# Adding the identity to the diagonal blocks of W1 and W2: accumulating DMAs in place of GpSimd tensor operations

## The chip, the core and the metric

The kernel runs on one core of one Trainium2 chip. The metric is the device time in microseconds (us) of one execution. Three executions of the kernel before took 483.61, 483.93 and 484.32 us, a median of 483.93 us. All views below are of one profiled execution of it.

## What is computed

Four residual layers follow each other on `x` of 8 batches by 256 rows by 1024 columns, in float32:

```
x = x + quantise(x)                       # L0: 8 groups of thresholds, deltas, zero points
x = x + einsum('bsi,boi->bso', x, W1[ids_a[b]])   # L1: one of 8 matrices 1024x1024, by batch
x = x + einsum('bsi,oi->bso', x, W2) + 0.5 * (x @ lora_A[ids_b[b]]) @ lora_B.T      # L2
x = x + (x @ B[ids_a[b]].T) @ A[ids_a[b]].T       # L3, rank 16
```

`x + x W` is computed as `x (W + I)`: each layer's residual is folded into its matrix by adding 1 to the diagonal. That addition is what the change touches.

## The kernel before

The rows of a batch are two halves of 128 (`t` = 0 and 1); a half is a "unit", of which there are 16. The five engines run programs of their own, written out by hand, which wait for one another on semaphores.

**ScalarE and VectorE (ACT, DVE)** walk through steps `n`, eight to a unit, one for each quantisation group. In a step ACT scales and rounds (`multiple`, L329, into the ring `tq` of 4) and makes a mask (`exceeds`, L344), and DVE takes the magic number off (`value`, L439), clamps (`clamp`, L448) and selects into `y` (`select`, L460). After a unit's last step `close_unit` (L468, L475) writes `x1`, the input of layer 1. Other work is put between the steps by tables of step numbers. Those that matter here are `ACT_W2` = steps 9 to 16, at which ACT rounds a slice `k` of W2 to `w2h` (L400), `DVE_W2` = steps 10 to 13 and 18 to 21, at which DVE takes the rest `w2l` (L513), and `ACT_X2`/`DVE_X2`, at which the result of layer 1 is split into `x2h` (L353) and `x2l` (L481).

**TensorE (PE)** first prepares the small adapter tables, then goes through the batches (`batch`). For each half it multiplies `x1` by `w1b` (`w1_x1`, L603, eight output tiles `o`, two to a pair `j`) and then `x2` by W2 (`product`, L628, in three terms: `w2h` by `x2h`, `w2h` by `x2l`, `w2l` by `x2h`). Before it uses pair `j` of W1 for the first half it waits for `w1_ready`. The first batch is written out, batches 1 to 6 are a loop (`pe.Fori`), the last is written out again. In each trace a float32 matmul of L603 leaves two records.

**SyncE (SP)** issues all loads and stores. W1 of a batch comes in four pairs of 1 MB into `w1b`, each as soon as PE has finished with the pair of the batch before (`w1_used`). W2 comes once, in eight slices of 512 KB, into a ring `stage` of `ST` = 4 buffers (`ua` and three of `ring`). Slice `k` + 4 can be loaded only when DVE has made `w2l` of slice `k` (`load_w2`, L211).

**GpSimd (POOL)** has one job after its two memsets: it adds `eye` (the identity, 128x128) to the diagonal blocks. `w2_diagonal(k)` (L290) waits for the load of slice `k`, and adds to one block of 128x128. `w1_diagonal(b, j)` (L295) waits for the load of pair `j` of batch `b`, and adds to two such blocks. For batch 0 the two kinds alternate; for batches 1 to 7 a loop does the four pairs. ACT waits for `w2_diag` before `w2h` of slice `k`. In a fragment:

```
if n in ACT_W2:
    k = ACT_W2.index(n)
    act.wait_ge(w2_diag, k + 1)
    nc.scalar.activation(w2h[:, k, :], stage[k % ST], ACT.Copy).then_inc(w2h_ready, 1)
```

Of the kernel before, what the change touches and what calls it, by code (L numbers as in the profile page):

```python
# [5 lines left out]
def quantised_residual_adapter_stack(nc, x, params, w1, w2t, w2n, b3t, b2n, b2r, a3, la, ids_b, ids_a,  # L6
# [9 lines left out]
    ALU = mybir.AluOpType  # L16
    ACT = mybir.ActivationFunctionType

    P = 128
    B, _, UN, KT, _ = x.shape  # L20
    T = UN * P
    OT = KT
# [11 lines left out]
    PAIRS = OT // 2  # L34
# [8 lines left out]
    TQ, MK, ST = 4, 2, 4  # L43

    ctx = ExitStack()
    with ctx:
        def sb(name, shape, dt=f32):
            return ctx.enter_context(nc.sbuf_tensor(name, shape, dt))
# [4 lines left out]
        def sem(name):  # L53
            return ctx.enter_context(nc.semaphore(name))
# [34 lines left out]
        eye = sb("eye", [P, P])  # L89
# [41 lines left out]
        y_ready = sem("y_ready")  # L131
        y_cut = sem("y_cut")
        x1_ready = sem("x1_ready")
        w1_ready = sem("w1_ready")
        w1_used = sem("w1_used")
        bank0_done = sem("bank0_done")
        acc_done = sem("acc_done")
        out_ready = sem("out_ready")
        w2_diag = sem("w2_diag")
        x2h_ready = sem("x2h_ready")  # L140
        x2l_ready = sem("x2l_ready")
        vh_ready = sem("vh_ready")
# [24 lines left out]
        def e_place(e):  # L167
            h, half = divmod(e, 2)
            return outb[:, h, half * DH:(half + 1) * DH]
# [111 lines left out]
        @block.gpsimd  # L281
        def _(pool):
            nc.gpsimd.memset(v_hl[:, :, :].bitcast(f32), 0.0).then_inc(pads, 1)
            nc.gpsimd.memset(u_hl[:, :].bitcast(f32), 0.0).then_inc(pads, 1)
            pool.wait_ge(b_in, 64)

            def w2_diagonal(k):
                pool.wait_ge(stage_in[k % ST], 16 * (k // ST + 1))
                diag = stage[k % ST][:, k * P:(k + 1) * P]
                nc.gpsimd.tensor_tensor(diag, diag, eye[:, :], ALU.add).then_inc(w2_diag, 1)  # L290

            def w1_diagonal(b, j):
                pool.wait_ge(w1_in[j], 16 * (b + 1))
                diag = w1b[:, 2 * j:2 * j + 2, 0:P]
                nc.gpsimd.tensor_tensor(diag, diag, eye[:, :].unsqueeze(1).to_broadcast([P, 2, P]), ALU.add) \  # L295
                    .then_inc(w1_ready, 1)

            for j in range(PAIRS):
                w1_diagonal(0, j)
                w2_diagonal(j)  # L300
            for k in range(PAIRS, KT):
                w2_diagonal(k)
            with pool.Fori(1, B) as b:
                for j in range(PAIRS):
                    w1_diagonal(b, j)

# [15 lines left out]
        def _(act):  # L322
# [67 lines left out]
            def tables(n):  # L390
                if n == ACT_G:
                    act.wait_ge(g_tiles, KT)
                    for i in range(2):
                        nc.scalar.activation(gsb[:, :, i * HALF:(i + 1) * HALF, :],
                                             g_bank[i][:, :].rearrange("p (i a r) -> p a i r", i=HALF, a=NA),
                                             ACT.Copy).then_inc(g_ready, 1)
                if n in ACT_W2:
                    k = ACT_W2.index(n)
                    act.wait_ge(w2_diag, k + 1)
                    nc.scalar.activation(w2h[:, k, :], stage[k % ST], ACT.Copy).then_inc(w2h_ready, 1)  # L400
                for e in range(2 * EH):
                    if n == ACT_E[e]:
                        act.wait_ge(e_done, 2 * EH)
                        nc.scalar.activation(e_place(e), e_bank[e][:, :], ACT.Copy).then_inc(e_ready, 1)  # L404
# [4 lines left out]
            for n in range(END):  # L409
                if n < STEPS:  # L410
                    multiple(n)
                if 2 <= n < STEPS + 2:
                    exceeds(n - 2)
                for i in range(2):
                    c, off = divmod(n - ACT_X2[i], G)
                    if off == 0 and 0 <= c < UN * B:
                        round_x2(c, i)
                for b in range(B):
                    s = n - PER * b
                    if s == ACT_V:  # L420
                        round_v(b)
                    if s in (ACT_U, ACT_U + 1):
                        round_u(b, s - ACT_U)
                    if s == ACT_LOW:
                        round_low(b)
                    for q in range(ACCS):
                        if s == ACT_OUT[q] and b < LAST:
                            finish_out(b, q)
                tables(n)
# [132 lines left out]
        def _(pe):  # L562
# [32 lines left out]
            def w1_x1(b, t, tiles):  # L595

                for o in tiles:
                    if t == 0 and o % 2 == 0:
                        pe.wait_ge(w1_ready, PAIRS * b + o // 2 + 1)
                    i = o // HALF  # L600
                    for k in range(KT):
                        at = (k - o) % KT * P
                        last = nc.tensor.matmul(x2_bank[2 * t + i][:, o % HALF * P:(o % HALF + 1) * P],  # L603
                                                w1b[:, o, at:at + P], x1[:, t, k, :],
                                                start=(o % HALF == 0 and k == 0), stop=(k == KT - 1),
                                                skip_group_check=True)
                    if t == 0 and o % HALF == HALF - 1:
                        last.then_inc(bank0_done, 1)
                    if t == 1 and o % 2 == 1:
                        last.then_inc(w1_used, 1)  # L610
# [34 lines left out]
            def batch(b, first=False, last=False):  # L645
                pe.wait_ge(x1_ready, UN * b + 1)
                if first:
                    w1_x1(b, 0, range(OT))
                else:
                    w1_x1(b, 0, range(U_AT))  # L650
                    for q in range(ACCS):
                        u_low(b - 1, q)
                    w1_x1(b, 0, range(U_AT, OT))
# [100 lines left out]
```

## Time and profile before

| | |
|---|---|
| median of 3 runs | 483.93 us (483.61 to 484.32) |
| profiled execution, first to last instruction (span) | 481.9 us |
| what the median has beyond that span | 2.0 us |
| PE / DVE / ACT / POOL busy | 464.9 / 419.4 / 358.6 / 45.5 us |
| POOL: 32 additions for W1, 8 for W2 | 36.5 us and 7.0 us of the 45.5 |
| mean DMA rate | 139 GB/s |

The profile gives no total time of its own for the profiled execution beside its span, so the 2.0 us is the difference to the median of other runs. "Busy" is time in which an instruction of the engine was being executed. A row of a timeline reads: start in us from the start of the span, duration in us, engine, line, operation, what it writes and reads, sizes and count, and in brackets how long the engine stood idle before and what released it.

### The profile page before, as it was taken

How to read it: one execution, taken by the hardware profiler on the slowest of the kernel's cores; microseconds unless marked ns; L12 is line 12 of the kernel's file. 1: busy time of each engine (PE TensorE's matmuls, PEld its weight loads, DVE VectorE, ACT ScalarE, POOL GpSimd, SP SyncE). 2: the span in 40 equal slices, each digit the busy share in tenths (PEclk: the TensorE clock that was granted, in tenths of full speed). 3: DMA queues.
4: the chain of work that ended last, by engine and by line, in shares of the span. 5: the costliest groups of instructions: out<-in, count | busy, mean ns of one | idle time of the engine just before them, and what ended most of it. 6: DMA issues, size and time to landing. Idle time of an engine off the chain costs nothing.

```text
span 481.9 us, 8215 instructions
## 1 busy us (share of the span) xinstructions
PE 464.9 (96%) x3184; PEld 424.7 (88%) x3184; DVE 419.4 (87%) x481; ACT 358.6 (74%) x383; POOL 45.5 (9%) x46
## 2 busy tenths in 40 slices
PE   3999869999999999999999999999999999999997
PEld 3969669898999989898999989898999989898995
DVE  5999999999999899989999899989999899989120
ACT  6979958678877879678877879678887879675011
POOL 1064000200002000200002000210003000100000
PEclk9999989999999999999999999999999999999999
DMA  7997214712335122712335122712335122702002
GB/s 282 407 415 258 113 34 149 294 54 97 131 127 212 44 95 97 294 44 103 131 120 218 44 89 101 294 44 103 131 101 237 44 86 104 294 2 88 1 1 87
DMA packets 17830, 67.07 MB, mean 139 GB/s; under 512 B 2576, under 2 KB 5904, under 8 KB 13712
## 3 DMA queue, kind: packets, MB, share of 16 engines
q1 hardware_dynamic: 17808, 66.81, 37.9%
q8 instruction: 10, 0.16, 0.2%
q14 instruction: 12, 0.10, 0.1%
HBM read 56.84 MB, written 9.96 MB: 139 GB/s over the span
## 4 chain that ended last, share of the span: by engine, by line
PE 90%; ACT 3%; DMA 3%; DVE 2%; issue 1%; POOL 1%; SPq 0%; DVEq 0%
PE x_bank L603 45%; PE acc L628 34%; PE acc L579 3%; PE x_bank L616 3%; PE acc L640 2%; PE acc L638 2%; DMA w1b<-w 2%; DMA rows<-own_rows 1%; ACT mask L344 1%; ACT w2h L400 1%; DVE y L460 1%; PE acc L567 1%; ACT tq L329 1%; PE acc L577 0%; ACT outb L404 0%
## 5 line engine op out<-in xcount | busy, mean ns | idle before, releaser
L603 PEld LDWEIGHTS x_bank<-x,w1b 128*128 128x128 f32 x2048 | 233.2, 193 | 8.2 <-issue 4.9
L603 PE MATMUL x_bank<-x,w1b 128*128 128x128 f32 x2048 | 234.8, 276 | 3.7 <-DVE x L475 3.7
L344 ACT ACTIVATE mask<-absx,negtop 128x1024 bf16<-128x1024 f32 x112 | 128.4, 1146 | 40.3 <-DVE y L460 39.5
L329 ACT ACTIVATE tq<-xin,magic,rdelta 128x1024 f32<-128x1024 f32 x128 | 157.0, 1234 | 0.6 <-DVE yhigh L526 0.3
L460 DVE COPY_PREDICATED y<-mask,uq 128x1024 f32<-128x1024 int16 x112 | 151.1, 1349 | 0.1
L439 DVE TENSOR_SCALAR tq<-tq,par 128x1024 f32<-128x1024 f32 x128 | 99.2, 775 | 3.7 <-DVE y L460 3.1
L448 DVE TENSOR_SCALAR uq<-tq,ylow,yhigh 128x1024 f32<-128x1024 f32 x112 | 92.3, 824 | 0.2 <-DVE y L460 0.2
L628 PE MATMUL acc<-w2h,x2h 128*128 128x512 f32 x256 | 80.9, 393 | 2.0 <-DVE x2l L481 2.0
L628 PE MATMUL acc<-w2h,x2l 128*128 128x512 f32 x256 | 79.9, 390 | 0.0
L628 PE MATMUL acc<-w2l,x2h 128*128 128x512 f32 x256 | 79.2, 390 | 0.0
L295 POOL TENSOR_TENSOR w1b<-w1b,eye 128x256 f32<-128x256 f32 x32 | 36.5, 1140 | 368.9 <-DMA w1b<-w 368.9
L628 PEld LDWEIGHTS acc<-w2h,x2l 128*128 128x128 f32 x256 | 48.1, 188 | 10.3
L628 PEld LDWEIGHTS acc<-w2l,x2h 128*128 128x128 f32 x256 | 48.0, 188 | 10.2
L628 PEld LDWEIGHTS acc<-w2h,x2h 128*128 128x128 f32 x256 | 46.3, 188 | 10.6 <-DVE x2l L481 2.4
L481 DVE TENSOR_TENSOR x2l<-x_bank,x2h 128x512 fp32r<-128x512 f32 x32 | 22.1, 690 | 35.5 <-ACT x2h L353 35.5
L353 ACT ACTIVATE x2h<-x_bank 128x512 fp32r<-128x512 f32 x32 | 18.9, 592 | 28.1 <-PE x_bank L603 27.8
L337 ACT ACTIVATE absx<-xin 128x1024 f32<-128x1024 f32 x15 | 15.9, 1063 | 21.9 <-DVE uq L468 21.9
L388 ACT ACTIVATE outb<-acc 128x512 f32<-128x512 f32 x32 | 18.1, 598 | 7.5 <-PE acc L640 7.5
L468 DVE SCALAR_TENSOR_TENSOR uq<-absx,top,y 128x1024 f32<-128x1024 f32 x16 | 23.2, 1448 | 0.6
L475 DVE TENSOR_TENSOR x<-xin,uq 128x1024 f32<-128x1024 f32 x16 | 19.4, 1215 | 0.0
L579 PE MATMUL acc<-x,w1b 128*128 128x128 f32 x128 | 16.8, 288 | 0.0
L616 PE MATMUL x_bank<-x2h,v_hl 128*128 128x256 f32 x64 | 16.3, 289 | 0.0
(57 smaller groups left out, 218.9 us busy)
## 6 DMA issues: line engine op xcount, KB each, us to landing
w1b<-w SPq DMA_DIRECT2D x32, 1024.0 KB, 6.7
xin<-x SPq DMA_DIRECT2D x16, 512.0 KB, 3.7
out<-outb SPq DMA_DIRECT2D x14, 512.0 KB, 2.8
w1b<-w2n SPq DMA_DIRECT2D x4, 1024.0 KB, 10.6
ring<-w2t SPq DMA_DIRECT2D x6, 512.0 KB, 6.7
ua<-e_dram SPq DMA_DIRECT2D x16, 128.0 KB, 2.5
ua<-w2t SPq DMA_DIRECT2D x2, 512.0 KB, 7.8
va<-la SPq DMA_DIRECT2D x8, 128.0 KB, 2.7
```

Of the source, the lines that this page charges most:

```text
L295: nc.gpsimd.tensor_tensor(diag, diag, eye[:, :].unsqueeze(1).to_broadcast([P, 2, P]), ALU.add) \
L329: nc.scalar.activation(tq[:, n % TQ, :], flat(xin, c % UN), ACT.Identity, bias=magic[:, 0:1], scale=rdelta[:, g:g + 1]).then_inc(t_ready, 1)
L344: nc.scalar.activation(mask[:, n % MK, :], absx[:, :], ACT.Relu, bias=negtop[:, g:g + 1], scale=1.0).then_inc(mask_ready, 1)
L439: nc.vector.tensor_scalar(tq[:, n % TQ, :], tq[:, n % TQ, :], -MAGIC, par[:, 1, g:g + 1], ALU.add, ALU.mult).then_inc(u_ready, 1)
L448: nc.vector.tensor_scalar(clamped_y, tq[:, n % TQ, :], ylow[:, g:g + 1], yhigh[:, g:g + 1], ALU.max, ALU.min).then_inc(clamped, 1)
L460: nc.vector.copy_predicated(y[:, :], mask[:, n % MK, :].bitcast(i16), uq[:, n % 2, :]) \
L468: nc.vector.scalar_tensor_tensor(ycut, absx[:, :], top[:, G - 1:G], y[:, :], ALU.is_gt, ALU.mult).then_inc(y_cut, 1)
L481: nc.vector.tensor_tensor(x2l[:, t, tiles, :].rearrange("p k t -> p (k t)"), x2_bank[2 * t + i][:, :], x2h[:, t, tiles, :].rearrange("p k ...
L579: last = nc.tensor.matmul(into, w2g[:, i, o * P:(o + 1) * P], b3s[:, o, :], start=False, stop=(o == OT - 1))
L603: last = nc.tensor.matmul(x2_bank[2 * t + i][:, o % HALF * P:(o % HALF + 1) * P], w1b[:, o, at:at + P], x1[:, t, k, :], start=(o % HALF == ...
L616: last = nc.tensor.matmul(low_bank[:, 0:T], v_hl[:, k, :], xs[:, :, k, :], start=(k == 0 and xs is x2h), stop=(k == KT - 1 and xs is x2l), ...
L628: nc.tensor.matmul(acc[2 * t + h][:, :], xs[:, t, k, :], w[:, k, h * DH:(h + 1) * DH], start=(k == 0 and xs is x2h and w is w2h), stop=Fal ...
```

## The change

The tensor operations of `w2_diagonal` and `w1_diagonal` become DMAs, issued by GpSimd, that read `eye` from the core's memory and add it to the block in place (`accum_op=ALU.add`). Since a DMA raises its semaphore by 16 in pieces, each W1 pair and each stage buffer gets a semaphore of its own. The waits of ACT and PE are rewritten to match, and GpSimd's loop over the batches is written out.

```
-        w1_ready = sem("w1_ready")
+        w1_ready = [sem(f"w1_ready{j}") for j in range(PAIRS)]
-        w2_diag = sem("w2_diag")
+        w2_diag = [sem(f"w2_diag{c}") for c in range(ST)]
...
             def w2_diagonal(k):
                 pool.wait_ge(stage_in[k % ST], 16 * (k // ST + 1))
                 diag = stage[k % ST][:, k * P:(k + 1) * P]
-                nc.gpsimd.tensor_tensor(diag, diag, eye[:, :], ALU.add).then_inc(w2_diag, 1)
+                pool.dma_start(diag, eye[:, :], accum_op=ALU.add).then_inc(w2_diag[k % ST], 16)
...
                 diag = w1b[:, 2 * j:2 * j + 2, 0:P]
-                nc.gpsimd.tensor_tensor(diag, diag, eye[:, :].unsqueeze(1).to_broadcast([P, 2, P]), ALU.add) \
-                    .then_inc(w1_ready, 1)
+                pool.dma_start(diag, eye[:, :].unsqueeze(1).to_broadcast([P, 2, P]), accum_op=ALU.add) \
+                    .then_inc(w1_ready[j], 16)
...
-            with pool.Fori(1, B) as b:
+            for b in range(1, B):
                 for j in range(PAIRS):
                     w1_diagonal(b, j)
...
-                    act.wait_ge(w2_diag, k + 1)
+                    act.wait_ge(w2_diag[k % ST], 16 * (k // ST + 1))
...
-                        pe.wait_ge(w1_ready, PAIRS * b + o // 2 + 1)
+                        pe.wait_ge(w1_ready[o // 2], 16 * (b + 1))
```

GpSimd's program from the end of its memsets on, before (a `w1b` row is a pair of W1, a `ua` or `ring` row a slice of W2):

```order
L284 MEMSET u_hl 128x1024
L295 ISA
L295 TENSOR_TENSOR w1b<-w1b,eye 128x2x128
L290 TENSOR_TENSOR ua<-ua,eye 128x128
L295 TENSOR_TENSOR w1b<-w1b,eye 128x2x128
L290 TENSOR_TENSOR ring<-ring,eye 128x128
L295 TENSOR_TENSOR w1b<-w1b,eye 128x2x128
L290 TENSOR_TENSOR ring<-ring,eye 128x128
L295 TENSOR_TENSOR w1b<-w1b,eye 128x2x128
L290 TENSOR_TENSOR ring<-ring,eye 128x128
L290 TENSOR_TENSOR ua<-ua,eye 128x128
L290 TENSOR_TENSOR ring<-ring,eye 128x128 x3
```

The same stretch now:

```order
L284 MEMSET u_hl 128x1024
L295 DMA w1b<-eye 128x2x128
L290 DMA ua<-eye 128x128
L295 DMA w1b<-eye 128x2x128
L290 DMA ring<-eye 128x128
L295 DMA w1b<-eye 128x2x128
L290 DMA ring<-eye 128x128
L295 DMA w1b<-eye 128x2x128
L290 DMA ring<-eye 128x128
L290 DMA ua<-eye 128x128
L290 DMA ring<-eye 128x128 x3
L295 DMA w1b<-eye 128x2x128 x28
```

The places and their order are the same; each addition has become a DMA, and the 28 of batches 1 to 7 follow without a loop.

TensorE's program at the head of the loop over batches 1 to 6, where it begins on a new W1, before:

```order
L599 ISA
L603 MATMUL x_bank<-x,w1b 128x128 x16
L599 REGISTER_ALU
L603 MATMUL x_bank<-x,w1b 128x128 x8
L638 MATMUL acc<-u_hh,low_hc 128x512
L640 MATMUL acc<-u_hl,low_lh 128x512
```

and now:

```order
L599 ISA
L603 MATMUL x_bank<-x,w1b 128x128 x24
L638 MATMUL acc<-u_hh,low_hc 128x512
L640 MATMUL acc<-u_hl,low_lh 128x512
```

No matmul has moved. The register additions that made each wait's number are gone from between them, since all four pairs now wait for the same number.

## Rows read from the trace of the kernel before

**Rows 1.** Page, chain that ended last: share of the span by engine.

```profile
PE 90%; ACT 3%; DMA 3%; DVE 2%; issue 1%; POOL 1%; SPq 0%; DVEq 0%
```

**Rows 2.** Waits, whole span: total us, times, longest us.

```profile
PE x_bank L603 <- DVE x L475: 3.7, 1, 3.7
...
ACT w2h L400 <- POOL ua L290: 2.8, 1, 2.8
...
PEld x_bank L603 <- DVE x L475: 2.2, 6, 0.4
```

**Rows 3.** Chain in order of time, stretch 25 to 66 us: start, us, what.

```profile
38.44 0.87 POOL ring L290
39.34 1.06 ACT w2h L400
...
54.84 0.49 ACT x2h L353
55.35 0.69 DVE x2l L481
...
64.28 1.15 DVE x L475
```

**Rows 4.** Timeline of ACT, the slices k = 0 and k = 4 of W2.

```profile
28.65 1.06 ACT L400 ACTIVATE w2h<-ua 128x1024 fp32r<-128x1024 f32 x1 [2.83 <-POOL ua L290]
...
42.95 1.04 ACT L400 ACTIVATE w2h<-ua 128x1024 fp32r<-128x1024 f32 x1
```

**Rows 5.** Timeline of POOL, the slices k = 0 and k = 4.

```profile
27.71 0.90 POOL L290 TENSOR_TENSOR ua<-ua,eye 128x128 f32<-128x128 f32 x1
...
42.00 0.52 POOL L290 TENSOR_TENSOR ua<-ua,eye 128x128 f32<-128x128 f32 x1 [2.69 <-DMA ua<-w2t]
```

**Rows 6.** Timeline of SP's DMA issues: slices k = 0, 3 and 4.

```profile
17.82 0.43 SPq L211 DMA_DIRECT2D ua<-w2t  x1
...
29.86 0.43 SPq L211 DMA_DIRECT2D ring<-w2t  x1
...
35.16 0.33 SPq L211 DMA_DIRECT2D ua<-w2t  x1
```

**Rows 7.** DMA issues from 17 to 30 us: count, KB each, median us to landing.

```profile
ring<-w2t SPq DMA_DIRECT2D x3, 512.0 KB, 8.4
ua<-w2t SPq DMA_DIRECT2D x1, 512.0 KB, 8.9
```

**Rows 8.** DMA issues from 35 to 46 us.

```profile
ua<-w2t SPq DMA_DIRECT2D x1, 512.0 KB, 6.8
...
vg<-g_dram SPq DMA_DIRECT2D x1, 64.0 KB, 3.7
```

**Rows 9.** All 8 loads of tile vg (64 KB each).

```profile
DMA to landing us min/median/max: 1.9/2.4/3.7
```

**Rows 10.** Timeline, DVE: first w2l, and L468 with POOL idle and busy.

```profile
33.38 1.75 DVE L513 TENSOR_TENSOR w2l<-ua,w2h 128x1024 fp32r<-128x1024 f32 x1
...
120.20 1.29 DVE L468 SCALAR_TENSOR_TENSOR uq<-absx,top,y 128x1024 f32<-128x1024 f32 x1
...
146.38 1.61 DVE L468 SCALAR_TENSOR_TENSOR uq<-absx,top,y 128x1024 f32<-128x1024 f32 x1
```

**Rows 11.** Timeline, POOL and PE: pair 1 of batch 1, and its use.

```profile
90.93 1.83 POOL L295 TENSOR_TENSOR w1b<-w1b,eye 128x256 f32<-128x256 f32 x1 [8.01 <-DMA w1b<-w]
...
96.27 5.62 PE L603 MATMUL x_bank<-x,w1b 128*128 128x128 f32 x48
```

**Rows 12.** POOL's additions for W1, all 32: min/median/max ns.

```profile
L295 POOL TENSOR_TENSOR w1b<-w1b,eye x32: 730/1001/2153, 25.6 to 422.1; 128x256 f32<-128x256 f32 x32
```

**Rows 13.** Stretches: length, busy PE, PEld, DVE, ACT, POOL; granted clock, DMA share, GB/s.

```profile
62.00:65.50 3.50, 0.00 (x0) 0.00 (x0) 3.43 (x5) 2.00 (x2) 0.00 (x0) 1.00 0.00 0
...
67.00:69.00 2.00, 2.00 (x12) 2.00 (x11) 2.00 (x4) 1.91 (x2) 0.00 (x0) 0.50 0.33 98
```

**Rows 14.** Chain in order of time: second half of batch 0 and of batch 1.

```profile
65.56 16.16 PE x_bank L603 x128
...
123.57 14.51 PE x_bank L603 x128
```

## The prediction

> **What bounds the kernel now.** I read the chain that ended last first, then the waits, then the timelines of the head. The chain lies on PE for 90% of the span [rows 1]. PE's waits show where it isn't PE: it stands still once for 3.7 us, for `x1` of the second unit, and its weight loads wait 2.2 us in all, six times, for the same line later on [rows 2]. GpSimd appears among the long waits once: ACT stood 2.8 us for the first slice of W2 [rows 2]. So two stretches are to be looked at. The head, up to PE's start on the second half at 65.56 us [rows 14], is where W2 is prepared and ACT and DVE set the pace. The batches after it, where PE does, are where only W1's additions take place.
>
> **The head, followed back.** The chain there goes from POOL's addition to slice k = 3, which ends at 39.31 us, to ACT's `w2h` at 39.34, then along ACT to `x2h` at 54.84, to DVE's `x2l` at 55.35, and along DVE to `x1` at 64.28 plus 1.15, for which PE has been waiting [rows 3]. A reader should see two things. ACT takes `w2h` of k = 3 0.03 us after POOL is done, so there is no reserve at that slice. And nothing on the chain between 39.34 and 65.43 is a transfer or a free engine: what ACT loses at a slice of W2 arrives at PE in full.
>
> **What the change does to the head.** Call A the time from the landing of a slice to the moment ACT sees its diagonal done. Now that is one POOL operation: 0.90 us at k = 0, 0.52 us at k = 4 [rows 5]. After the change it is the issue by GpSimd, the transfer of 64 KB within the core's memory, its addition, and the semaphore.
> - k = 0: issued by SP at 17.82, landed 8.9 us later, so at 26.7 [rows 6, 7]. ACT began at 28.65, having waited [rows 4]. ACT is delayed by 26.7 + A - 28.65, that is A - 1.9.
> - k = 3: issued at 29.86 [rows 6], landing by the median of its kind, 8.4 us [rows 7], at 38.3. ACT began at 39.34 [rows 3]. Delay A - 1.1.
> - k = 4: issued at 35.16 [rows 6], landed 6.8 us later [rows 8], at 42.0, where POOL took it up [rows 5]. ACT began at 42.95 [rows 4]. Delay A - 0.95.
>
> These are delays of one chain, so the largest counts, not their sum: D = A - 1.0. The later slices have several us between their addition and ACT's use and don't bind. This holds while the stage ring isn't held up in turn. Slice 4 can be loaded only after DVE's `w2l` of slice 0, which began at 33.38 [rows 10] where `w2h` of slice 0 was done at 28.65 + 1.06 = 29.7 [rows 4]: 3.7 us of reserve. With A - 1.9 above 3.7, so A above 5.6, each further microsecond counts about twice, once for slice 0 and again for slice 4.
>
> **The size of A.** The trace has no DMA of GpSimd and no accumulating one. The nearest rows are SP's loads of 64 KB: 1.9 us at the least, 2.4 at the median and 3.7 us in this very stretch, with other loads in flight [rows 8, 9]. From below A is 1.9 us; nothing lets a transfer that must first read both operands be quicker than the quickest plain one of its size. From above it is 8.9 us, what a load takes when it queues behind a full megabyte [rows 7]; the additions have a queue of their own. I take 3.7 us, the row nearest in size and stretch, and 0.7 us for a slower issue and the second operand. That 0.7 is my choice; half of it to three times it would do as well. A = 4.4 and D = 3.4 us.
>
> The Trainium skill ("DMA: Bandwidth & Descriptors", "Where the ~2 µs actually goes" and "Latency and other measured facts") gives about 2.0 us of fixed cost for a DMA issued by GpSimd and about 1 us to its first byte. By that, as an estimate from the page, A would be some 3.2 us and D 2.2; no run here shows a GpSimd DMA yet.
>
> **What the change does to the batches.** Each of the 28 additions becomes a DMA of 128 KB. The tightest is pair 1. It has landed by 90.93, when POOL takes it up, and PE needs it after two of three output tiles of the stretch that starts at 96.27 and lasts 5.62, so at 100.0 [rows 11]: 9.1 us for A. With A = 4.4 nothing waits. POOL's queue holds nothing else, so no one stands behind a slow issue except the next pair, which is needed later still. In batch 0 the pairs have about as much. Cost zero, covered by PE's work on the tiles before; the cover ends at A = 9.1.
>
> **What else is removed or added.** POOL's 36.5 us for W1 and 7.0 us for W2 of work go; nobody but ACT at k = 0 waited for them [rows 2]. They do slow DVE: L468 takes 1.29 us with POOL idle and 1.61 beside an addition, the first `w2l` 1.75 us [rows 10]. In the head that gives DVE back about 1 us, but ACT is what the chain runs on, so the gain is zero. In the batches DVE's gain is lost in its own wait for the next `x2h`. The register additions on PE lay between queued matmuls; zero. The traffic added is 6 percent of a megabyte load per slice and 13 per pair; zero.
>
> **Sum.** The span goes from 481.9 to 485.3 us. With the 2.0 us that the median of the runs lies above the span, 487.3 us, or 3.4 over the median of 483.93. A difference of 0.2% (about 0.97 us) is what a measurement of this kernel can tell from none.
>
> **Rivals.**
> 1. *DVE is freed and PE gets its x1 sooner* (faster). PE's weight loads wait for L475 six times, 2.2 us in all [rows 2], and additions of POOL stretch the DVE operations that lead to such an `x1`, as at 146.38 [rows 10]. If those waits are DVE's fault and the additions are what makes DVE late, up to 2.2 us go: 481.7 us. Against it: the waited-for `x1` is that of the second half, before which POOL is idle, and the head would have to cost nothing, so A would have to be 1.0 us or less, half the quickest load. It decides only at A below about 2. Chance 0.07.
> 2. *The head absorbs it* (no change). A is near its lower bound of 1.9 us, D = 0.9, and 484.8 us or less comes out. Chance 0.10.
> 3. *The clock moves.* PE stood idle from 62.0 to 65.5 us, and after it the granted clock was 0.50, the 1.2 GHz level of its two, at 67 to 69 us [rows 13]; that is why the stretch at 65.56 took 16.16 us where the one at 123.57 took 14.51 [rows 14], a loss of 1.65 us. With D = 3.4 PE also gets a longer pause, of some 3.5 us, before `x2l` at 55.35. If the clock falls there instead, PE's slower work eats into its later pause, and the 1.65 us may not be lost: 485.6 us. Chance 0.10.
> 4. *Starved descriptors.* GpSimd has to write the descriptors of its DMAs, and POOL's work is stretched up to threefold by what DVE does beside it: the same addition takes from 730 to 2153 ns [rows 12], and DVE is busy nearly all the time. Were the issue alone 5 us and A 10, the head would lose 9 us and the second-order 4.4 (A above 5.6), and each of 7 batches 0.9: some 504 us. A up to 7 is in my range. Chance of more than the range 0.08.
>
> On rival 4 the Trainium skill ("SBUF — State Buffer", "Who interferes with whom") speaks against this change: a DMA that appears to be stalled by DVE is one of GpSimd's, kept from writing its descriptors while DVE holds the shared port pair. The rows show the stretching of POOL's additions, but not yet that of a DMA's issue.
>
> The forecast itself, A from 2.3 to 7, holds the remaining 0.65.
>
> **Range and chances.** A = 7 gives, with the second order, 26.7 + 7 - 28.65 = 5.05 at slice 0, 1.4 of it past the reserve, so D = 6.0 + 1.4 = 7.4: 491.3 us. Below, D = 0.9 less a little gives 484.6, and rival 3 lies inside. I take 484.6 to 491.5; rival 1, half of rival 2 and the end of rival 4 stay outside, 0.20 in all. Faster by over 0.2%: 0.07. Within 0.2%, 483.0 to 484.9: rival 2 and a few cases in which the clock gives back most of a small D, 0.13. Slower: 0.80.
>
> **What the new profile would show.** If right: ACT waits for W2's DMAs some 3 us more than its 2.8 in the head, one wait of 1 to 3 us at slice 1, 3 or 4; `x1` of the second unit ends near 68.8 in place of 65.4; PE's wait before it stays near 3.7 us; from there to the end every stretch is as long as before, and DVE's L468 is 1.29 us throughout. The length of the issue on POOL and the time to landing would give A. It is wrong if PE waits for `w1_ready` in batches 1 to 7, if `x1` of the second unit isn't later, or if the stretch from PE's start on the second half to the end differs by more than 1 us from 481.9 - 65.6 = 416.3 us.

## The result, and the profile after

The changed kernel takes 494.63 us (median of 6 runs, 493.86 to 495.94), beside 483.91 us (6 runs, 483.61 to 484.79) for the kernel before. The ratio is 1.0189, with a 95% interval of 1.0156 to 1.0221: slower by 10.7 us. The forecast was 487.3 us in a range of 484.6 to 491.5. The direction was right; the forecast loss of 3.4 us was a third of the true one, and the time lies outside the range. All six runs of the kernel before lie between 483.6 and 484.8 us here; beside the experiments it has a second level near 487.0, which is taken up there.

The profiled execution has a span of 493.2 us, 11.3 more than the 481.9 of before. Its page, with the chain by engine that answers to [rows 1], and the queues:

```profile
span 493.2 us, 8191 instructions
PE 470.1 (95%) x3184; PEld 429.3 (87%) x3184; DVE 408.1 (83%) x481; ACT 357.8 (73%) x383; POOL 55.6 (11%) x46
...
q1 hardware_dynamic: 17808, 66.81, 37.3%
q0 software_dynamic: 9856, 4.72, 8.1%
...
PE 86%; DMA 7%; ACT 3%; DVE 2%; issue 1%; SPq 1%; DVEq 0%
```

DVE is 11.3 us less busy than before and the span is 11.3 us longer: none of DVE's gain reached the end. The chain now lies on DMAs for 7% of the span where it was 3%. A queue that before did not exist, GpSimd's q0, moves 4.72 MB in 9856 packets. The waits, to be read beside [rows 2], name the place:

```profile
ACT w2h L400 <- DMA ua<-eye: 12.1, 2, 11.0
...
PEld acc L628 <- DVE x2l L481: 8.3, 2, 7.0
...
DVE w2l L513 <- ACT w2h L400: 6.5, 2, 5.0
...
PE x_bank L603 <- DVE x L475: 3.7, 1, 3.7
...
PEld x_bank L603 <- DVE x L475: 2.1, 6, 0.4
```

ACT stands 11.0 us at once for the first slice of W2, where it stood 2.8. PE's last wait of the head, 3.7 us, and its six short ones, 2.1 us, are as before. The chain in order of time, from the load of slice 0 to `x2l`, is to be laid beside [rows 3]:

```profile
19.18 7.69 DMA ua<-w2t
26.87 0.30 issue
27.17 9.60 DMA ua<-eye
...
36.78 1.06 ACT w2h L400
...
39.97 0.40 SPq L230
...
41.03 7.92 DMA ua<-w2t
48.95 0.28 issue
49.24 3.91 DMA ua<-eye
...
65.58 0.69 DVE x2l L481
```

SP's first load of W1 left 1.4 us later in this execution than in the one before (18.79 against 17.43), ahead of anything the change touches; but slice 0 landed at 26.87 against 26.7, so this is no part of the loss. Two accumulating DMAs stand in the chain, and they are of the same size. The first, at slice 0, needs 9.60 us from its issue on GpSimd to its landing; the second, at slice 4, 3.91. Between them stands a step of SP that was not on the chain before: L230, the store of the adapter table, ahead of the load of slice 4. That load also has to wait for DVE's `w2l` of slice 0, which now runs as soon as ACT is done with the slice:

```profile
37.87 1.23 DVE L513 TENSOR_TENSOR w2l<-ua,w2h 128x1024 fp32r<-128x1024 f32 x1 [5.04 <-ACT w2h L400]
```

It ends at 39.10, where before it ended at 35.13 [rows 10].

ACT's timeline at slices 0, 1 and 4 gives the delay at each:

```profile
36.78 1.06 ACT L400 ACTIVATE w2h<-ua 128x1024 fp32r<-128x1024 f32 x1 [11.01 <-DMA ua<-eye]
...
40.82 1.06 ACT L400 ACTIVATE w2h<-ring 128x1024 fp32r<-128x1024 f32 x1 [0.88 <-DMA ring<-eye]
...
53.17 1.06 ACT L400 ACTIVATE w2h<-ua 128x1024 fp32r<-128x1024 f32 x1 [1.09 <-DMA ua<-eye]
```

Against 28.65, 31.80 and 42.95 before, ACT is late by 8.1, 9.0 and 10.2 us. The last of these is made up of four parts: the load of slice 4 is issued 5.9 us late (4.0 for `w2l` of slice 0, 1.9 for what SP has in front of it), takes 1.1 us longer to land, and its addition takes 4.2 us to reach ACT in place of 0.95. Nothing is added after slice 4: `x1` of the second unit is ready at 75.67 in place of 65.43, again 10.2 us late. From there on:

```profile
75.80 17.43 PE x_bank L603 x128
...
134.96 14.47 PE x_bank L603 x128
```

PE's first stretch takes 17.43 us where [rows 14] have 16.16, and the later ones are as before (14.47 and 14.51). From PE's start on the second half to the end of the span it is 417.4 us, against 416.3. The account is 10.2 us in the head and 1.3 us of clock just behind it, less 0.2 elsewhere: 11.3.

The clock shows in the windows:

```profile
62.00:66.00 4.00, 3.43 (x9) 2.31 (x8) 2.70 (x6) 4.00 (x5) 0.00 (x0) 0.65 0.32 128
66.00:75.50 9.50, 5.74 (x24) 4.42 (x24) 9.22 (x10) 6.75 (x7) 0.00 (x0) 0.98 0.00 0
75.50:80.00 4.50, 4.20 (x20) 4.23 (x21) 4.50 (x7) 3.86 (x4) 0.00 (x0) 0.50 0.32 89
```

PE now has two pauses after which it runs at the lower of its two levels, 1.2 GHz: one of 6.8 us before 58.62, and the old one of 3.7 us before 75.80. The first slow stretch costs nothing, because PE waits afterwards anyway. The second costs what the longer stretch of 17.43 us shows: the granted clock is 0.50 up to about 81.8 us, 6 us after the start, where before it was back at 0.96 at 69 to 71 us, some 3.5 us after. It goes with the length of the new pause: in e2, e3, e5 and e8 below, where PE stood 4.8 to 5.5 us before its first `x2l`, this stretch takes 16.16 us as before; in e4 and the change, with 6.6 and 6.8 us, it takes 17.14 and 17.43. What lies behind that is not shown.

### The profile page after: what moved, and what is told of

Same layout as the page of the kernel before. It is cut to its first block, busy times and chain, and to the rows that moved or that the text cites. A ratio compares the mean times of both kernels' runs of the same rounds, so it can differ in the third digit from the quotient of the medians.

```text
span 493.2 us, 8191 instructions
## 1 busy us (share of the span) xinstructions
PE 470.1 (95%) x3184; PEld 429.3 (87%) x3184; DVE 408.1 (83%) x481; ACT 357.8 (73%) x383; POOL 55.6 (11%) x46
## 3 DMA queue, kind: packets, MB, share of 16 engines
q1 hardware_dynamic: 17808, 66.81, 37.3%
q0 software_dynamic: 9856, 4.72, 8.1%
## 4 chain that ended last, share of the span: by engine, by line
PE 86%; DMA 7%; ACT 3%; DVE 2%; issue 1%; SPq 1%; DVEq 0%
PE x_bank L603 44%; PE acc L628 34%; DMA ua<-w2t 3%; PE x_bank L616 3%; DMA ua<-eye 3%; PE acc L640 2%; PE acc L638 1%; PE acc L579 1%; DMA rows<-own_rows 1%; DVE y L460 1%; PE acc L567 1%; ACT tq L329 1%; ACT mask L344 1%; ACT w2h L400 1%; ACT outb L404 0%
## 5 line engine op out<-in xcount | busy, mean ns | idle before, releaser
L439 DVE TENSOR_SCALAR tq<-tq,par 128x1024 f32<-128x1024 f32 x128 | 95.8, 749 | 3.7 <-DVE y L460 3.1
L448 DVE TENSOR_SCALAR uq<-tq,ylow,yhigh 128x1024 f32<-128x1024 f32 x112 | 90.9, 811 | 1.6 <-ACT mask L344 1.4
L628 PE MATMUL acc<-w2h,x2h 128*128 128x512 f32 x256 | 82.7, 401 | 7.7 <-DVE x2l L481 7.7
L295 POOL DMA_DIRECT2D w1b<-eye x32 | 46.3, 1447 | 366.8 <-DMA w1b<-w 366.8
L628 PE MATMUL acc<-w2h,x2l 128*128 128x512 f32 x256 | 81.2, 395 | 0.0
L628 PEld LDWEIGHTS acc<-w2h,x2l 128*128 128x128 f32 x256 | 49.1, 192 | 10.7
L628 PEld LDWEIGHTS acc<-w2l,x2h 128*128 128x128 f32 x256 | 48.0, 188 | 10.2
L468 DVE SCALAR_TENSOR_TENSOR uq<-absx,top,y 128x1024 f32<-128x1024 f32 x16 | 20.6, 1285 | 0.6
L579 PEld LDWEIGHTS acc<-x,w1b 128*128 128x128 f32 x128 | 17.1, 214 | 0.0
## 6 DMA issues: line engine op xcount, KB each, us to landing
w1b<-w2n SPq DMA_DIRECT2D x4, 1024.0 KB, 10.8
```

The source lines that it names most:

```text
L295: pool.dma_start(diag, eye[:, :].unsqueeze(1).to_broadcast([P, 2, P]), accum_op=ALU.add) \
L439: nc.vector.tensor_scalar(tq[:, n % TQ, :], tq[:, n % TQ, :], -MAGIC, par[:, 1, g:g + 1], ALU.add, ALU.mult).then_inc(u_ready, 1)
L448: nc.vector.tensor_scalar(clamped_y, tq[:, n % TQ, :], ylow[:, g:g + 1], yhigh[:, g:g + 1], ALU.max, ALU.min).then_inc(clamped, 1)
L468: nc.vector.scalar_tensor_tensor(ycut, absx[:, :], top[:, G - 1:G], y[:, :], ALU.is_gt, ALU.mult).then_inc(y_cut, 1)
L579: last = nc.tensor.matmul(into, w2g[:, i, o * P:(o + 1) * P], b3s[:, o, :], start=False, stop=(o == OT - 1))
L628: nc.tensor.matmul(acc[2 * t + h][:, :], xs[:, t, k, :], w[:, k, h * DH:(h + 1) * DH], start=(k == 0 and xs is x2h and w is w2h), stop=Fal ...
```

## The experiments

Eleven kernels ran besides the change. Five of them put tensor operations back at some slices or pairs, two move or hold back loads, one copies without adding, and three are the kernel before again.

**A word on the reference.** Beside the experiments the kernel before falls on two levels, about 483.8 and 487.0 us, within one set of runs (13 runs beside the first four variants: 5 from 483.69 to 483.96, 8 from 485.89 to 487.22; over all three sets 17 and 22 of 39). Against the upper level the change is 7.6 us slower and not 10.7. Ratios below are to all runs of before in the same set, so their intervals are wide, and conclusions about 3 us rest on rows of the traces, of one execution each. The last experiments look for what makes the two levels.

### Which additions cost: W1's or W2's

```
e1:  w1_diagonal: DMA as in the change;  w2_diagonal: nc.gpsimd.tensor_tensor(diag, diag, eye, ALU.add)
e2:  w2_diagonal: DMA as in the change;  w1_diagonal: nc.gpsimd.tensor_tensor(...)
```

> Only W1's 32 additions are DMAs; W2's eight are GpSimd tensor operations again, each on its old semaphore. Theory (the whole loss is W2's diagonals in the head, where ACT waits for them): the time is that of the kernel before, 483.9 us, perhaps up to 0.8 less, since DVE is slowed less. Rival 1 (the added DMA traffic and GpSimd issue cost something in every batch): at least 485.5. Rival 2 (W1's pairs of batch 0, which took 9 to 11 us to land, hold PE up): 486 or more.

> Only W2's eight additions are DMAs; W1's are tensor operations again. Theory A (the addition of slice 0 is slow because its packets share the DMA engines with SP's loads): it still takes about 9 us to land and the time is that of the change, 493 to 495 us. Theory B (it is slow because it stands behind W1's pair 0 in GpSimd's own queue, which landed 2 us before it): it lands in 7 us or less and the time falls to 489 to 492 us.

With W1 alone by DMA: 486.67 us (10 runs, 485.95 to 487.96), ratio 1.0024 (0.9999 to 1.0048), span 485.1. With W2 alone: 491.42 us (4 runs), ratio 1.0129 (1.0076 to 1.0181), span 489.4. So W2 carries most of the loss. Whether W1's DMAs cost anything depends on the level that they are held against: all ten runs of e1 lie at the upper one and none at the lower, so they are 2.9 us above the lower and level with the upper, and the interval of the ratio holds 1. The trace shows what holds e1 there. It isn't that PE waits for a pair (0.17 us, once); ACT waits for slice 4:

```profile
35.52 0.49 SPq L211 DMA_DIRECT2D ua<-w2t  x1
```

```profile
45.78 0.69 POOL L290 TENSOR_TENSOR ua<-ua,eye 128x128 f32<-128x128 f32 x1 [4.64 <-DMA ua<-w2t]
```

The first row is SP's issue, the second POOL's timeline. SP issues the load 0.36 us later than before; it lands after 10.2 us, where 6.8 was the figure of [rows 8]. The 6.8 is the shortest of its kind: in the other traces with no DMA of W1 in the head (e0, e7, e9, e10) the load took 7.6 to 8.3 us, and in those with them beside it (e1, e3, e8) 9.9 to 10.9. So W1's DMAs of batch 0, of which pairs 2 and 3 are in flight in that stretch, take some 2 to 3 us from it. Rival 2 named the wrong consumer but the right cause. In e2 the addition to slice 0 lands 6.5 us after its issue instead of 9.6:

```profile
34.11 1.06 ACT L400 ACTIVATE w2h<-ua 128x1024 fp32r<-128x1024 f32 x1 [8.43 <-DMA ua<-eye]
```

Both of theory B's numbers came out: some 3 us of the 9.6 come from W1's DMAs, of which pair 0, 128 KB, was issued 1.7 us earlier on GpSimd's queue and pair 1 2.5 us later; e2 takes away both. The remaining 6.5 do not. The 9.6 has a spread of its own: in e4, whose program is the same up to there, the same DMA took 11.1 us.

### Where in the program: head or batches

```
e7:  if b == 0: nc.gpsimd.tensor_tensor(...)      # W1 of batch 0, and all of W2
     else:      pool.dma_start(diag, eye..., accum_op=ALU.add)
```

> DMAs only for W1 of batches 1 to 7 (28 of the 40 additions); W1 of batch 0 and all of W2 are tensor operations. Theory (nothing is lost outside the head): no difference to the kernel before measured beside it, within 0.3%, and every PE stretch after the second half's start as long as in before. Rival (the 28 DMAs cost by their traffic): 1 us or more over before.

The measured time is 485.83 us (10 runs, 483.44 to 486.91), ratio 0.9989 (0.9957 to 1.0020), with the same kind of two levels as before; the profiled execution has a span of 481.7. The theory holds: 28 of the 40 additions, 70% of them, cost nothing that shows in this trace or in the ratio, whose interval reaches from 2.1 us faster to 1.0 us slower. Their times in this run:

```profile
DMA to landing us min/median/max: 3.1/4.2/5.9
```

All are below the 9.1 us of cover that the prediction found behind pair 1.

### Why slice 0's DMA is slow: the loads beside it, or the addition

```
e6:  SP:  if j == 1: sp.wait_ge(w2_diag[0], 16)   # holds the loads of pair 1 and all later ones
e5:  pool.dma_start(diag, eye...)                 # no accum_op, in all 40
```

> The change, but SP holds back all loads from pair 1 of W1 on until the addition to slice 0 of W2 is done. Theory (the addition took 9.6 us because SP's loads were in flight on the same DMA engines): it lands in 3 to 4.5 us. Rival (a GpSimd DMA is that slow at its first use, or because DVE is busy, or because it stands behind pair 0's): 7 us or more. The total time is of no interest, the later loads all come late.

> The change with plain copies in place of accumulating DMAs (the diagonal blocks become the identity instead of gaining it, so the output is another). Theory (queueing among SP's loads, not the addition, is the cost): slice 0's still takes 7 us or more and the time is within 2 us of the change's 494.6. Rival (reading the destination and adding is what is slow): slice 0's lands in 5 us or less, the time is 489 or less.

With SP's loads held back, the same DMA in the same place lands in 3.1 us (DMA issues of e6 from 25 to 28.2 us):

```profile
w1b<-eye POOLq DMA_DIRECT2D x1, 128.0 KB, 3.5
ua<-eye POOLq DMA_DIRECT2D x1, 64.0 KB, 3.1
```

9.6 us fell to 3.1 although GpSimd's queue still holds pair 0 in front and it is still the second DMA that GpSimd ever issues. So two thirds of those 9.6 us are what was in flight beside it: SP's loads, and pair 1's addition, which can't start before its load. How busy the DMA engines are does not price it alone. Their mean busy share during slice 0's 9.6 us was 1.09, and during the 3.9 us of slice 4's 0.86. (The kernel as a whole took 500.38 us in its one run; the later loads all come late, as intended.)

The plain copies lie between theory and rival: 490.67 us (4 runs), ratio 1.0102 (1.0050 to 1.0153), slice 0 in 6.0 us (DMA issues of e5, 25 to 28.2 us):

```profile
w1b<-eye POOLq DMA_DIRECT2D x1, 128.0 KB, 6.0
ua<-eye POOLq DMA_DIRECT2D x1, 64.0 KB, 6.0
```

So beside the same loads the addition itself adds 3.6 us to a copy that takes 6.0. The queue's row on the page of e5 says in what coin:

```profile
q0 software_dynamic: 1792, 4.72, 2.8%
```

For the same 4.72 MB the accumulating form moves 9856 packets and takes 8.1% of the DMA engines' time, the plain form 1792 packets and 2.8%. GpSimd's issue is longer too, 1.20 us at the median for a pair against 0.72.

### Do the delays of the slices add up

```
e3:  k < 4: tensor operation, on a semaphore of its own;   k >= 4, and all of W1: DMA
e8:  k == 0: tensor operation;                             all else: DMA
```

> The change with slice 0 of W2 alone added by a tensor operation. In the change ACT was late by 8.1 us at slice 0, and slice 1's addition landed 9.9 us after its issue, at 40.8 us, where ACT had taken slice 1 at 31.8 before. Theory (only the largest delay of the head's chain counts): taking slice 0 out of it saves 0 to 3 us, 491.5 to 494.5 us. Rival (the delays of the slices add up, slice 0's 8 us goes away): 486 to 488 us.

e8 measured 492.03 us (4 runs, 491.29 to 492.81), ratio 1.0113 (1.0075 to 1.0152). Slice 0 is early, and ACT stands at slice 1 instead:

```profile
27.72 1.06 ACT L407 ACTIVATE w2h<-ua 128x1024 fp32r<-128x1024 f32 x1 [1.70 <-POOL ua L292]
40.73 1.06 ACT L407 ACTIVATE w2h<-ring 128x1024 fp32r<-128x1024 f32 x1 [8.97 <-DMA ring<-eye]
```

Slice 1 is taken at 40.73, within 0.1 us of the changed kernel's 40.82; what e8 gains, 2.6 us, it gains behind it (slice 4 is loaded from 36.0 on and not from 41.0, and taken at 51.7). The 8 us at slice 0 vanished and the wait for it came back as one of 9.0 us at the next. Only the largest delay of the chain counts, as the prediction's sum had it.

> Slices 0 to 3 of W2 by tensor operations, slices 4 to 7 and all of W1 by DMAs. Theory (slice 0 in the saturated stretch makes 8 us of the loss, and slice 4 alone would cost its own A of about 4.2 less 1.0): 3.2 us over before, 487.1 us, range 486 to 488.5. Rival (the loss is in the later slices, through the stage ring): 491 or more.

e3 measured 491.59 us (4 runs), ratio 1.0127 (1.0077 to 1.0177), so my 487.1 was wrong. The rival's number came out, though not by its path, since the ring holds the load of slice 4 up by 0.7 us at most:

```profile
50.77 1.06 ACT L407 ACTIVATE w2h<-ua 128x1024 fp32r<-128x1024 f32 x1 [5.51 <-DMA ua<-eye]
```

Slice 4 is 7.8 us late on its own. SP issues it at 35.89, 0.7 us later than before, but the load lands after 9.9 us instead of 6.8, as in e1, with W1's DMAs beside it, and its addition then takes 5.0 us to reach ACT. I had counted the addition's latency alone. W1's traffic had already taken 2 to 3 us from the load.

### SP's order

```
e4:  load_w2(4) moved ahead of  sp.wait_ge(g_ready, 2); store of g_dram; load_x(1, 0)
```

> The change, but SP issues the load of slice 4 before it waits for the adapter table and stores it, and before the load of x. In the change that load left 5.9 us later than before. Theory (ACT is late by 9.0 us at slice 3 already, from slices 0 and 1, and slice 4 adds only about 1.1): 493.5 us, about 1 less than the change. Rival (SP's order is the bulk: the late load of slice 4 sets the end by itself): 490 or less.

e4 measured 493.33 us (4 runs, 492.78 to 493.64), ratio 1.0161 (1.0111 to 1.0210): the theory's 493.5. The load of slice 4 still leaves late, directly behind `w2l` of slice 0, which in e4 ends at 40.5:

```profile
40.54 0.33 SPq L211 DMA_DIRECT2D ua<-w2t  x1
```

Its addition is no longer what ACT waits for. ACT takes slice 4 as soon as it has done what comes before it:

```profile
48.58 1.04 ACT L400 ACTIVATE w2h<-ring 128x1024 fp32r<-128x1024 f32 x1
52.18 1.04 ACT L400 ACTIVATE w2h<-ua 128x1024 fp32r<-128x1024 f32 x1
```

There is no wait at 52.18, where the change waited until 53.17. SP's order is worth about 1 us: without it ACT is 9.2 us late at slice 4 from the slices before, with it 10.2.

### The two levels of the kernel before

> The kernel before, unchanged, for a trace from the chip on which the variants run; there its times fell on two levels, about 483.9 and 487.0 us, and all ten of W1-only's on one, 486.7. Theory: the upper level is a late landing of slice 4 of W2, 9 to 10 us after its issue where the first trace had 6.8, and ACT waits for it at the 9th to 13th step. Rival: the three microseconds lie in the batches or in the clock.

> The kernel before once more, for a trace of its upper level of about 487 us. Theory: if the run falls on it, slice 4 of W2 lands 9 to 10 us after its issue and ACT waits 2 to 3 us more in the head. Rival: the three microseconds lie elsewhere.

> The kernel before a second time, for the same purpose: theory and rival are those of the look before it, a late landing of slice 4 in the head or something elsewhere.

The first two profiled executions fell on the lower level (spans 482.4 and 482.1), the third on the upper, 486.94 us with a span of 485.1. Its POOL timeline at slice 4:

```profile
43.11 3.28 POOL L290 TENSOR_TENSOR ua<-ua,eye 128x128 f32<-128x128 f32 x1 [3.65 <-DMA ua<-w2t]
```

Its ACT timeline:

```profile
46.42 1.06 ACT L400 ACTIVATE w2h<-ua 128x1024 fp32r<-128x1024 f32 x1 [3.22 <-POOL ua L290]
```

The theory is refuted in its size: the load landed 8.3 us after an issue at 34.75 and not 9 to 10, so at 43.0, and POOL began at 43.11; in e9's, on the lower level, POOL began at 42.56. What is late is POOL's addition of 128x128. It took 3.28 us here and 0.60 in e9. DVE begins `x1` of the second unit at 67.65 here and at 64.69 in e9: 3.0 us late, about the distance of the two levels. DVE ran without a gap through that stretch:

```profile
42.93 0.82 DVE L448 TENSOR_SCALAR uq<-tq,ylow,yhigh 128x1024 f32<-128x1024 f32 x1
43.65 1.32 DVE L460 COPY_PREDICATED y<-mask,uq 128x1024 f32<-128x1024 int16 x1
44.85 1.22 DVE L513 TENSOR_TENSOR w2l<-ring,w2h 128x1024 fp32r<-128x1024 f32 x1
45.98 0.96 DVE L439 TENSOR_SCALAR tq<-tq,par 128x1024 f32<-128x1024 f32 x1
```

POOL's operation began 0.18 us after the first of these and ended inside the last. In e9 the order is the other way round, POOL first and the same `clamp` 0.18 us behind it, and there it is DVE's operation that is longer, 0.98 in place of 0.82 us:

```profile
42.56 0.60 POOL L290 TENSOR_TENSOR ua<-ua,eye 128x128 f32<-128x128 f32 x1 [3.30 <-DMA ua<-w2t]
42.74 0.98 DVE L448 TENSOR_SCALAR uq<-tq,ylow,yhigh 128x1024 f32<-128x1024 f32 x1
```

In e0 POOL is 0.20 us ahead of it and takes 0.59. So in these three traces half a microsecond in the landing goes with which of the two begins first, and that goes with the level. The Trainium skill ("SBUF — State Buffer", "Who interferes with whom") has a rule that fits: a VectorE instruction with two operands in SBUF, or in a two-port mode, and a GpSimd one that reads SBUF use one shared port pair, and the second to issue stands until the first is done. The rows agree with it in the order of the two starts, and DVE's own time was stretched beside POOL as [rows 10] show; but only one trace is of the upper level, and that the port was the cause was not tried apart.

## Why the prediction was wrong

- **What bounds the kernel, and that the head's delay arrives at PE in full: right.** Both `x1` and ACT's slice 4 are 10.2 us late, and PE's wait of 3.7 us before `x1` is unchanged.
- **"D = A - 1.0", the largest delay of one chain and not a sum: right in form.** e8 shows it, and with the 9.9 us of slices 0 and 1 the formula gives 8.9, where ACT was 9.0 late at slice 1. At slice 4 the A that the sum used, 4.4 us, is met almost exactly: landed at 48.95, taken at 53.17, 4.2 us.
- **"The size of A" is the step that failed: 4.4 us, where slices 0 and 1 took 9.9.** I took one A for all slices and priced it from the 64 KB load that started at 40.10 us. That is at the very end of the rush of loads: before, the DMA share was 1.00 to 1.04 from 26 to 42 us, and 0.44 from 42 to 46 (two of these stretches stand in the rows below; the share is the last figure but one). Slices 0 and 1 are added inside the rush. There A is 9.9 us at slice 0 (26.87 to 36.78), and slice 1 takes as long from the issue on POOL alone (30.93 to 40.82). Even the upper bound of 8.9 us, said to be excluded because the additions have a queue of their own, was passed. A queue of one's own doesn't keep one's packets from sharing the engines: e6 shows 3.1 us for the same DMA without the loads. The side estimate of 3.2 us for A fits the additions away from the rush: from issue to landing slices 5 to 7 took 2.4 to 3.3 us. The sum with the true A at slice 0 would have been 26.87 + 9.9 - 28.65 = 8.1 us there, and the measured delay is 8.1.

```profile
38.00:42.00 4.00, 4.00 (x38) 4.00 (x37) 4.00 (x4) 3.90 (x6) 1.30 (x3) 1.00 1.00 392
42.00:46.00 4.00, 4.00 (x38) 4.00 (x38) 4.00 (x5) 4.00 (x7) 1.72 (x3) 1.00 0.44 158
```

- **"The traffic added is 6 percent of a megabyte load per slice and 13 per pair; zero": wrong.** Counted by bytes it is small. By packets it is 9856 against 17808 of SP's queue, and per MB an accumulating DMA takes three times the engine time (8.1% for 4.72 MB against 37.3% for 66.81 MB). In the head that moved slice 4's landing by some 2 to 3 us (e1, e3).
- **The second order: right, and by the path named, but not the whole of it.** DVE's `w2l` of slice 0 had 3.7 us of reserve, so a delay of 8.1 at slice 0 should make it 4.4 late; it began at 37.87, 4.5 late, and ended 4.0 late. The load of slice 4 left 5.9 us late. The other 1.9 is a wait that I had not asked about: SP stands in front of this load for `g_ready`, which ACT gives at the step before slice 1, behind slice 0, and issues a store and the load of `x` first. "No one stands behind" was asked of POOL's queue and not of SP's. e4 takes this second part away and gains 1.3 us.
- **What the batches cost: right, zero.** e7 shows it with 28 DMAs of 3.1 to 5.9 us, against a cover of 9.1. "In batch 0 the pairs have about as much" held only just: there they took 6.9 to 10.8 us. PE waited for none of them in the change, but 0.17 us for one in e1 and 0.43 in e3.
- **DVE's relief worth nothing: right.** L468 takes 1.28 to 1.29 us throughout, as expected, DVE is busy 11.3 us less, and PE's six waits total 2.1 us as before. Rival 1 falls with that.
- **Rival 3, the clock:** the new pause did bring a slow stretch, as supposed, but the old one stayed as well and got 1.27 us worse. The 1.65 us were not given back. Nor need it have helped: in e10 the stretch took 14.53 us, without the slow part, and PE then stood 1.58 us for the next `x1`; from PE's start on the second half to the end it is 416.1 us there and 416.0 in e9.
- **Rival 4, starved descriptors:** the issues on GpSimd took 0.86 to 2.35 us, never 5. It had the right size of A (10 us) for the wrong reason: the instruction that issues was not slow, and in e6 the DMA landed in 3.1 us with DVE busy for 98% of them, so DVE did not hold it up there; what was slow is what followed the issue among the loads. It was priced too high in the batches, where A stayed below 6.

Two things stay open: why the slow stretch grew, 1.3 us, and what makes an addition dearer than a copy. The 3.6 us between a plain copy and an addition in e5 may be their packets, five and a half times as many, or the reading of the destination; no run separates the two.

## What to carry to other kernels

A short DMA put in place of a short engine operation is priced by what is in flight on the DMA engines at that moment and in front of it on its own queue, so take the row of the same stretch of the program before that of the same size; here the same 64 KB took 3.1 us in quiet and 9.6 among megabyte loads. Count an accumulating DMA by its packets and not by its bytes, and ask what it takes from the loads around it. Where the wait for it has several microseconds of cover, as in the batches here, it costs nothing, and it gives nothing either if the engine it relieves isn't the bound.

## What the runs showed of the hardware that was not expected

- An accumulating DMA of 128 KB or 64 KB within the core's memory moves about 5.5 times the packets of a plain one (9856 against 1792 for 4.72 MB in all) and holds the DMA engines 2.9 times as long (8.1% against 2.8% of the span).
- A GpSimd tensor operation of 128x128 took from 0.45 to 3.28 us within one execution of the kernel before (e10), and the one of 3.28, on the chain, made the 3 us in the one trace of the upper level, 487.0 against 483.8 us. The six runs of the change stay within 2.1 us and show no such pair.
- SP's issue of a load can itself be held up. The load of `x` took 0.49 us to issue in the kernel before and 6.55 us in e6, where it came right behind six loads of 4.5 MB together, issued within 3 us (what it waited for is not shown):

```profile
34.51 6.55 SPq L175 DMA_DIRECT2D xin<-x  x1
```
